# Expert stages of a hybrid block: pool scatters y for two pairs of tiles per wait, with a y ring of eight pairs

## The reference

```python
def _L0_ffn_ref(x, router_w, router_bias, wg, wu, wd, swg, swu, swd):   # E, F, K = 64, 64, 4; D = 256
    flat = x.reshape(b * t, d)                                           # 4096 tokens
    logits = flat @ router_w
    scores = softmax(logits)
    _, topk_idx = top_k(logits + router_bias, K)
    topk_scores = scores taken at topk_idx, divided by their sum
    comb = topk_scores placed into [n, E]
    g = silu(einsum('nd,edf->nef', flat, wg))
    u = einsum('nd,edf->nef', flat, wu)
    routed = einsum('ne,nef,efd->nd', comb, g * u, wd)
    shared = the same for two shared experts of width 256
    return routed + shared

x = x + time_mix(layernorm(x)); x = x + ffn(layernorm(x))
x = x + retention(layernorm(x)); x = x + ffn(layernorm(x))
```

## Time and profile before

| | us |
|---|---|
| median of 3 runs | 2220.6 (2218.07 to 2226.54) |
| profiled execution, span from the first to the last instruction | 2224.4 |
| expert stage of the first mixture, first PE instruction to last scatter's issue | 644.7 to 991.0 |
| expert stage of the second mixture, last scatter's issue | to 2155.5 |
| PE busy / DVE busy / POOL busy in the span | 1603.3 / 1206.4 / 1031.6 |

### The profile page before, as it was taken

One profiled execution on the slowest core, in us unless ns is written; L12 is line 12 of the kernel. 1 busy time (PEld: TensorE's weight loads), 2 busy tenths in 40 slices (PEclk: granted clock), 3 DMA queues, 4 the chain that ended last, 5 costly groups with the idle time before them and its releaser, 6 DMA issues. The chain is left out here.

```text
span 2224.4 us, 28543 instructions
## 1 busy us (share of the span) xinstructions
PE 1603.3 (72%) x7784; PEld 1137.1 (51%) x7785; DVE 1206.4 (54%) x2657; ACT 448.9 (20%) x861; POOL 1031.6 (46%) x945
## 2 busy tenths in 40 slices
PE   5665358933778888867898989668933779898950
PEld 2333255511456666643767667555511457676740
DVE  6988778700124544434868686678600135445439
ACT  2333232100022222212020211132000022222210
POOL 3555632877015555552433426232777025555440
PEclk9878657965788888877999999858965888778775
DMA  9400000353154444406323330000443054444319
GB/s 369 186 0 0 0 32 3 113 227 119 30 121 140 135 131 141 120 21 237 116 115 114 114 114 1 4 30 13 162 181 122 15 147 145 133 125 133 107 43 349
DMA packets 132781, 245.12 MB, mean 110 GB/s; under 512 B 24370, under 2 KB 94054, under 8 KB 132212
## 3 DMA queue, kind: packets, MB, share of 16 engines
q1 hardware_dynamic: 101460, 176.74, 25.3%
q0 software_dynamic: 30720, 67.74, 8.2%
q10 hardware_dynamic: 544, 0.00, 0.0%
HBM read 121.38 MB, written 139.74 MB: 117 GB/s over the span
## 5 line engine op out<-in xcount | busy, mean ns | idle before, releaser
L1024 POOL DMA_INDIRECT pairs_y<-arena x384 | 380.1, 990 | 481.4 <-DVE arena L1124 359.6
L792 POOL DMA_INDIRECT slots_x<-arena x256 | 268.2, 1048 | 81.2 <-issue 79.1
L1057 PE MATMUL moe_eh<-arena 128*128 128x128 f32 x1536 | 256.4, 321 | 60.6 <-DVE arena L1116 56.1
L1057 PEld LDWEIGHTS moe_eh<-arena 128*128 128x128 f32 x1536 | 235.0, 234 | 70.0 <-ACT arena L1088 65.5
L1129 DVE TENSOR_TENSOR arena<-arena,moe_eh 64x256 f32<-64x256 f32 x192 | 81.2, 423 | 330.3 <-PE moe_ey L1068 208.5
L1068 PE MATMUL moe_ey<-arena 64*128 x768 | 258.4, 464 | 1.3 <-DVE arena L1137 1.3
L645 PE MATMUL moe_gate<-arena 128*128 (+1 forms) x256 | 139.7, 664 | 79.4 <-issue 41.1
L1068 PEld LDWEIGHTS moe_ey<-arena 64*128 64x128 f32 x768 | 152.4, 220 | 47.8 <-issue 14.8
L658 PE MATMUL moe_tp<-arena 128*128 128x256 f32 x512 | 123.8, 401 | 69.9 <-issue 67.3
L1046 PE MATMUL moe_ext<-ident,arena 128*128 128x128 f32 x768 | 146.3, 321 | 34.6 <-DMA arena<-slots_x 24.1
L1088 ACT ACTIVATE arena<-moe_ext 128x512 f32<-128x512 f32 x192 | 114.6, 597 | 268.5 <-PE moe_ext L1046 180.6
(11 more groups left out here) (199 smaller groups left out, 2372.0 us busy)
## 6 DMA issues: line engine op xcount, KB each, us to landing
slots_x<-empty_slots SPq DMA_DIRECT2D x96, 520.0 KB, 8.6
arena<-slots_x SPq DMA_DIRECT2D x192, 260.0 KB
arena<-pairs_y SPq DMA_DIRECT2D x64, 512.0 KB
arena<-w_gu SPq DMA_DIRECT2D x2, 8192.0 KB
pairs_y<-arena POOLq DMA_INDIRECT x384
residual<-x SPq DMA_DIRECT2D x4, 1024.0 KB
slots_x<-arena POOLq DMA_INDIRECT x256
out<-residual SPq DMA_DIRECT2D x4, 1024.0 KB, 9.0
```

What stands on the lines that cost most here:

```text
L792: pool.indirect_dma_start(out=slots.x, in_=xn[:, t, :], in_offset=None, out_offset=bass.IndirectOffsetOnAxis(ap=slot[:, t, i:i + 1], axis=0))\
L1024: pool.indirect_dma_start(out=slots.y, in_=ytile[:, n % YRING, j, :], in_offset=None, bounds_check=slots.pairs - 1, oob_is_err=False, out_ ...
L1057: last = pe.matmul(h_ps[place % 2][:, j * P:(j + 1) * P], weights[:, place % 2, j, h, :], xt[:, place % 2, (j * KH + h) * P:(j * KH + h + ...
```

## The change

Pool's loop goes over batches of two pairs: it waits once for the numbers and the y copies of both, then issues four indirect DMAs. The ring `ytile` has eight places instead of four. The copy of the pair numbers moves from the step after the load (before the multiply L1129) to the step of the y copy, just ahead of it and behind its wait for the ring; the pair numbers thus leave `xin` two steps later. The steps written out are sixteen instead of eight, and the hardware loop starts with the third round. To make room, `sig` moves onto the partitions 64 to 127 of the region whose lower partitions hold the down weights, and `empty_slots` holds one row of 260 floats instead of four; the zeroing DMAs read that row four times, so the same 520 KB are made of pieces of 1040 bytes.

```diff
-    XRING, YRING = 8, 4
+    XRING, YRING = 8, 8
+    BATCH = 2
...
-    sig = arena.take(2, 2 * P)
+    sig = arena.take(2, 2 * P, at=0)
...
-            for s in range(RING):
-                step(0, s, s)
-            with engine.Fori(1, NP // RING) as g:
+            for s in range(2 * RING):
+                step(s // RING, s % RING, s)
+            with engine.Fori(2, NP // RING) as g:
...
-                if s is None:
-
+                if s is None or s >= XRING:
                     sp.wait_ge(sem("xt_full"), n + 1 - XRING)
                     sp.wait_ge(sem("numbers_kept"), n + 1 - XRING)
...
-            for n in range(NP):
-                pool.wait_ge(sem("numbers_kept"), n + 1)
-                pool.wait_ge(sem("y_read"), 2 + n + 1)
-                for j in range(2):
-                    pool.indirect_dma_start(
+            for first in range(0, NP, BATCH):
+                pool.wait_ge(sem("numbers_kept"), first + BATCH)
+                pool.wait_ge(sem("y_read"), 2 + first + BATCH)
+                for n in range(first, first + BATCH):
+                    for j in range(2):
+                        pool.indirect_dma_start(
...
-                    dve.wait_ge(sem(f"x_in{place}"), 16 * turn + 16)
-                    dve.tensor_copy(goes_to[:, place, :], xin[:, place, :, D].bitcast(I32)).then_inc(sem("numbers_kept"), 1)
                     dve.wait_ge(sem("sig_ready"), n + 1)
...
-                        dve.wait_ge(sem(f"y_out{place % YRING}"), 32 * (RING // YRING * turn + place // YRING))
-                    dve.tensor_copy(ytile[:, place % YRING].rearrange("p j d -> p (j d)"), y_ps[place % 2][:, :])\
+                        dve.wait_ge(sem(f"y_out{place}"), 32 * turn)
+                    dve.wait_ge(sem(f"x_in{place}"), 16 * turn + 16)
+                    dve.tensor_copy(goes_to[:, place, :], xin[:, place, :, D].bitcast(I32)).then_inc(sem("numbers_kept"), 1)
+                    dve.tensor_copy(ytile[:, place].rearrange("p j d -> p (j d)"), y_ps[place % 2][:, :])\
...
-        self.zero = sb("empty_slots", [P, 4 * (256 + Slots.TAIL)], F32)
+        self.zero = sb("empty_slots", [P, 256 + Slots.TAIL], F32)
...
-        rows = self.slots.x.rearrange("(n p r) d -> n p (r d)", p=P, r=4)
+        rows = self.slots.x.rearrange("(n p r) d -> n p r d", p=P, r=4)
+        zeros = self.zero[:, :].unsqueeze(1).to_broadcast([P, 4, self.slots.width])
```

More of the change, by code:

```diff
@@ L1019, in _ @@
         def _(pool):
-            for n in range(NP):
-                pool.wait_ge(sem("numbers_kept"), n + 1)
-                pool.wait_ge(sem("y_read"), 2 + n + 1)
-                for j in range(2):
-                    pool.indirect_dma_start(
[L1025 to L1028, removed]
+            for first in range(0, NP, BATCH):
[4 more added lines that the diff above has]
+                        pool.indirect_dma_start(
+                            out=slots.y, in_=ytile[:, n % YRING, j, :], in_offset=None, bounds_check=slots.pairs - 1,
+                            oob_is_err=False, out_offset=bass.IndirectOffsetOnAxis(
+                                ap=goes_to[:, n % XRING, j:j + 1], axis=0))\
+                            .then_inc(sem(f"y_out{n % YRING}"), 16)
         @block.tensor
@@ L1799, in __init__ @@
         self.slots_zeroed = ctx.enter_context(nc.semaphore("slots_zeroed"))
-        floats = 43008
+        floats = 44224
         self.arena = Arena(sb("arena", [P, floats], F32), floats)
@@ L1805, in zero_slots @@
         sp.wait_ge(self.const_ready, self.CONSTS)
-        rows = self.slots.x.rearrange("(n p r) d -> n p (r d)", p=P, r=4)
+        rows = self.slots.x.rearrange("(n p r) d -> n p r d", p=P, r=4)
+        zeros = self.zero[:, :].unsqueeze(1).to_broadcast([P, 4, self.slots.width])
         for n in range(self.ZEROINGS) if parts is None else parts:
-            sp.dma_start(rows[n], self.zero[:, :]).then_inc(self.slots_zeroed, 16)
+            sp.dma_start(rows[n], zeros).then_inc(self.slots_zeroed, 16)
     def make_constants(self, pool):
@@ L1824, in make_constants @@
                            pattern=[[1, P]], channel_multiplier=-1).then_inc(self.const_ready, 1)
-        pool.memset(self.zero[:, :].rearrange("p (r d) -> p r d", r=4)[:, :, 256:], Slots.NO_PAIR)\
+        pool.memset(self.zero[:, 256:], Slots.NO_PAIR)\
             .then_inc(self.const_ready, 1)
```

## The result

The changed kernel takes 2280.97 us (median of 4 runs, 2275.72 to 2284.88), the kernel before beside it 2220.6 (2218.07, 2220.6, 2226.54). A fourth execution of the kernel before took 4941.71 us and is not counted. The ratio is 1.0272, interval 1.0247 to 1.0297: slower, by 60 us. A second comparison, on another chip, gave 1.0283 (1.0246 to 1.0320).

The account below looks back on a forecast made before the run. PE was taken as the bound, with about 95 us of idleness and half pace in each expert stage. Longer scatter strings (+32) and stage ends (+5), on the median 2220.6, gave 2258 us, range 2178 to 2305.

Parts of the forecast that it names:

- Strings of four and eight only, and eights hold PE longer: POOL's back-to-back scatters in the expert stages: no other lengths; PE's idle grows from 2.8 us at six to 5.4 at eight.
- One sign: Expected in the changed profile: ACT and DVE start together 1 us after a string of POOL's scatters ends.
- The sum for the strings, +32: Expert stages: PE's loss from longer runs of back-to-back scatters, +32 us in both, set between +24 and +40.
- two sums: PE's loss in both expert stages: +40 us from idle PE alone, +24 with half pace behind each long hold.
- The second sum: Both expert stages: +24 us, counting 6.6 us of half pace behind each long hold, with eights fewer than sixes.
- The share, three quarters of the fast pairs in eights: Of 51 first-stage pairs in strings of six or four at PE's fast clock, three quarters would lie in strings of eight.
- Ends of the stages, +5: At each expert stage's end POOL starts one pair later, 2.6 us a stage, +5 us in both.
- Ring, numbers, zeroing, written steps, 0 together: Eight-place ring, later number copy, smaller zeroing pieces and sixteen written steps: each taken as 0 us.
- The covers: Later x loads stay hidden five steps ahead, zeroing beside the time-mix and retention layer: both 0 us.
- Short strings: Rival, chance 0.29: held signals get out in pauses, POOL's strings stay at four in the expert stages; all fours 2172 us.
- String length without effect: Rival, chance 0.20: something else holds PE's signals, so only the ends of the stages count; 2226 us.
- A twelve: Rival, chance 0.07: eights drift into strings of three batches, PE idles some 10 us each; all pairs so, 2340 us.

Follow-up runs that it names:

- e1: The changed kernel with POOL waiting for one pair at a time again, all other parts kept: 2239.87 us, ratio 1.0071.
- e2: The kernel before with one edit, POOL waits for two pairs and then issues their four scatters: 2287.29 us, ratio 1.0293.
- e3: The changed kernel with four pairs per wait instead of two: 2354.8 us, ratio 1.058.
- e4: Scatter of y left out, POOL idle in the expert stages, SP stores y in slot order by plain DMA; no longer computes the layer: 2073.69 us, ratio 0.9329.
- e10: The changed kernel with POOL clearing 1040 numbers on 64 partitions and waiting for it after each two-pair batch, on a signal-holding chip: 2198.07 us, ratio 0.9955.
- e9: The changed kernel as it stands, on another chip that holds signals: 2273.47 us beside 2207.32 for the kernel before, ratio 1.0283.
- e6: The kernel before with only the copy of the numbers moved late, on the chip that holds no signals: 1962.32 us, ratio 1.0035.
- e12: The changed kernel with one pair per wait and the numbers copied early again, on a chip that holds signals: 2215.47 us, ratio 1.0042.
- e11: The changed kernel with a POOL pause after each two-pair batch, clearing 520 numbers on 64 partitions, on a signal-holding chip: 2159.99 us, ratio 0.9786.

## Why the prediction was right, and where its sizes were not

The forecast was slower, 2258 us; measured, 2281, inside 2178 to 2305. The mechanism was right. The change is 60 us where 37 was forecast, and by e1 most of the missing 23 lies in the parts that were put at nothing. Point by point:

**Strings of four and eight only, and eights hold PE longer.** Right in kind, by e1, e2, e3, e4 and e10. The form was right too: PE idles 4.59 us at an eight, and 4.5 on the mean, where 5.4 was forecast. One sign was half wrong: ACT's copy does start about 1 us after the string (1.6), but DVE's multiply comes at 808.86, still within it, so some held signals do get through.

**The sum for the strings, +32.** Somewhat too small: e1 puts the strings and the ends of the stages together at 41 to 44, where 32 + 5 = 37 was forecast; e2, whose other parts are those of the kernel before, puts them at 65. I had two sums, +40 from idle PE alone and +24 if each long hold also brings its stretch of half pace, and stood between them. The idle PE was close, a little low: forecast were 9.6 eights of 5.4 us a stage, 52 us; there are twelve waits of 4.5 us, 54 us a stage on the mean. Ahead of the gate/up matmuls it grew by 51 us against the kernel before and by 33 against e1. The second sum lowered the price because eights would be fewer than the sixes were, so that less half pace would follow. This relief did not come. Long waits are not fewer (24 of over 1.2 us in both stages, 23 before), and with only the pairs per wait changed PE's busy time in the two stages stays as it was: 595.8 us in e1 and 595.4 in the changed kernel, 608.8 before and 607.9 in e2, while these two steps lengthen PE's part of the stages by 37 and 47 us. The granted clock shows eleven stretches at half pace inside the first stage before, 106 us, and twelve after, 123 us; in the second there are twelve and 133 us in both. The 13 us by which PE is less busy than in the kernel before are there in e1 already, and smaller in e9 (602.6 us, 6 less), so they are no relief by longer strings. The rule of the Trainium skill (TensorE: Matmul & The Clock Gate, "HAM oscillation"), that waits in a loop throttle again on each turn, agrees with this trace: 2.08 us behind the 4.59. What failed is the relief that I had worked out from fewer holds. The stages were to grow by 10 to 25 us each and grew by 29 and 20.

**The share, three quarters of the fast pairs in eights.** That was 38 of 96 pairs; it is 48. The chain of fast pairs is cut otherwise: an eight every six or eight pairs, whatever lay there before.

**Ends of the stages, +5.** Right: the last scatter ends 9.15 and 8.68 us after the last copy of y has ended, where it was 6.64 in both, so +4.5.

**Ring, numbers, zeroing, written steps, 0 together.** Failed, the largest miss in kind: e1 shows +0.7%, 16 us, for terms that were each put at nothing. For the numbers I had seen the 0.19 us by which POOL starts later and called it harmless since nobody waits for it; on a chip where POOL is the bound it costs 0.35% (e6). Here PE's idle time is 18 us longer in e1 than in e12, which points the same way and is not clear of what two chips differ by. That ring, zeroing or written steps cost 0.4% (e12) is measured, not explained. The covers themselves held: no load of x became late (PE's waits ahead of its transposes that end with slots_x are 23.4 us, before 24.1), nor did the zeroing, though zeroing took 10.2 us from issue to landing instead of 8.6. e2 warns against adding these parts up: without them the two pairs per wait cost as much as all together.

**The rivals.** Short strings were refuted for this kernel and shown for another: where a pause is forced (e10, e11) strings stay at four and the time is below that of before, 0.979 of it in e11 where that rival had said 2172/2220.6 = 0.978 for all fours. It failed here because 14 of the 48 batches of the first stage follow the one before after 0.30 us, without a pause. String length without effect is out. A twelve came once, at the end of the first stage.

## What to carry to other kernels

Where one engine issues indirect DMAs back to back, look at when the others take up finished work, and lay the timelines side by side: a queue that is never late itself can still set the pace. Grouping waits to save a semaphore wait made the bursts longer and cost 2 to 3% (e1, e2); cutting them with a deliberate gap made the kernel 2% faster than the one before. Before tuning against such an effect, time the kernel before on more than one chip, since here the gap pays on one kind and costs on the other.

## What the runs showed of the hardware that was not expected

Chips differ in this: on one of those used, strings of sixteen scatters held no signal at all and the kernel before took 1954 us; on the others long strings did and it took 2206 to 2221. Why was not found; the scatters themselves took 0.98 us on both.

A forced gap of 1.3 us behind every four scatters lets the held signals through (e11); shorter ones were not tried.

POOL's work slows DVE's copies beside it. A copy of the weights took 287 ns in e4, where POOL did nothing. Beside a scatter it took 332 ns on the mean before, and beside a clearing 1.49 us in e10 (22 copies of 384) and 0.72 in e11 (42 copies). Over all of them the mean was 310 ns before, 392 in e10 and 376 in e11. PE's waits ahead of the gate/up matmuls in e10 nearly all end with such a copy (30.1 of 32.1 us), so it may cost some of them; no run separates that.
